# Fused attention and mixture of experts: router logits and values from one matmul per token tile, other slots for the steps around it

## The reference, cut to what matters

```
zn  = (xn - mean) / sqrt(var + eps) * ln_w + ln_b
qkv = zn @ W_qkv + b_qkv                    # 16 heads of 8
s   = xn + softmax(q k^T / sqrt(8)) v @ W_proj + b_proj
logits  = xn @ Wr + br                      # 8 experts
weights = softmax over the two largest logits, 0 elsewhere
ffn = sum over e of weights[e] * (gelu(xn @ W1[e] + b1[e]) @ W2[e] + b2[e])
```

## Time and profile before

| | us |
|---|---|
| median of 3 runs (lowest, highest) | 1032.16 (1031.27, 1032.86) |
| the profiled execution, its own time | 1031.52 |
| its span | 1029.5 |
| TensorE busy (matmul) | 1008.1 |
| ScalarE busy | 859.4 |
| VectorE busy | 842.9 |
| GpSimd busy | 351.1 |

### The profile page before, as it was taken

How to read it: one execution, slowest core, us unless ns; L and a number is a source line. 1 busy time by engine, 2 the same in 40 slices (tenths; PEclk the granted TensorE clock), 3 DMA queues, 4 the chain that set the end, 5 groups by cost and what they waited for, 6 DMA issues and landing times.

```text
span 1029.5 us, 17024 instructions
## 1 busy us (share of the span) xinstructions
PE 1008.1 (98%) x5837; PEld 443.0 (43%) x5869; DVE 842.9 (82%) x1283; ACT 859.4 (83%) x1166; POOL 351.1 (34%) x432
## 2 busy tenths in 40 slices
PE   6999999999999999999999999999999999999998
PEld 4676666666666666667222222222222222222222
DVE  5757878878887887785799999999999999999953
ACT  7877667676767767666999999999999999999985
POOL 5795665656575565746200010001000001000010
PEclk9999999999999999999999999999999999999999
DMA  6542322315132231412421222122221222212113
GB/s 198 131 117 60 103 56 59 102 32 145 31 93 69 57 118 33 113 39 69 116 53 50 55 60 57 42 60 54 54 63 43 58 53 53 59 51 57 26 26 88
DMA packets 102955, 72.11 MB, mean 70 GB/s; under 512 B 25737, under 2 KB 87878, under 8 KB 102870
## 3 DMA queue, kind: packets, MB, share of 16 engines
q1 hardware_dynamic: 102870, 71.04, 26.5%
HBM read 53.12 MB, written 15.59 MB: 67 GB/s over the span
## 4 chain that ended last, share of the span: by engine, by line
PE 87%; DVE 5%; issue 2%; ACT 2%; POOL 0%; another core or an unknown queue 0%; DVEq 0%; ACTq 0%; POOLq 0%
PE psum L1044 22%; PE psum L1004 13%; PE psum L989 10%; PE psum L974 6%; PE psum L934 5%; PE psum L936 5%; PE psum L935 5%; PE psum L952 5%; PE psum L960 4%; PE psum L957 4%; PE psum L958 4%; DVE neg_max_half L1321 1%; DVE neg_max_half L1295 1%; DVE neg_max_half L1291 1%; ACT p_ring L855 1%
## 5 line engine op out<-in xcount | busy, mean ns | idle before, releaser
L855 ACT ACTIVATE p_ring<-psum 128x1024 f32<-128x1024 f32 x512 | 494.5, 1031 | 19.6 <-PE psum L1004 9.1
L1291 DVE TENSOR_REDUCE neg_max_half<-psum 128x2 f32<-128x1024 f32 x240 | 294.3, 1226 | 42.3 <-PE psum L989 34.2
L1044 PE MATMUL psum<-p_ring,v_sb 128*9 128x512 f32 x2048 | 267.6, 594 | 0.2 <-ACT o_sb L846 0.2
L1321 DVE TENSOR_REDUCE neg_max_half<-psum 128x1 f32<-128x512 f32 x304 | 200.0, 685 | 74.9 <-PE psum L974 60.2
L812 ACT ACTIVATE h_hi<-psum,cols 128x512 fp32r<-128x512 f32 x192 | 132.4, 690 | 114.8 <-PE psum L936 114.0
L670 POOL TENSOR_TENSOR h_lo<-h_split,h_hi 128x512 fp32r<-128x512 f32 x128 | 166.2, 1300 | 151.8 <-ACT h_split L815 151.4
L1004 PE MATMUL psum<-q_stack,k_stack 51*128 51x512 bf16 x1024 | 201.2, 385 | 1.3 <-ACT p_ring L855 0.7
L989 PE MATMUL psum<-k_max_stack,q_max_stack 48*128 48x512 bf16 x720 | 182.2, 378 | 1.1
L1004 PEld LDWEIGHTS psum<-q_stack,k_stack 51*128 51x128 bf16 x1024 | 49.1, 92 | 296.6 <-ACT p_ring L855 282.7
L1295 DVE TENSOR_REDUCE neg_max_half<-psum 128x1 f32<-128x512 f32 x240 | 161.2, 672 | 0.0
L624 POOL CAST neg_max_parts<-neg_max_rest 128x16 bf16<-128x16 f32 x32 | 6.5, 203 | 448.4 <-DVE neg_max_rest L1304 448.2
(11 more groups left out here) (121 smaller groups left out, 967.9 us busy)
## 6 DMA issues: line engine op xcount, KB each, us to landing
expert_w_bc<-expert_w_dram SPq DMA_DIRECT2D x64, 256.0 KB, 4.9
k_rows_dram<-qk_parts SPq DMA_DIRECT2D x24, 256.0 KB, 2.8
q_max_stack<-q_rows_dram SPq DMA_DIRECT2D x64, 96.0 KB, 2.5
k_max_stack<-k_rows_dram SPq DMA_DIRECT2D x64, 96.0 KB, 2.5
q_stack<-q_rows_dram SPq DMA_DIRECT2D x64, 96.0 KB, 2.5
k_stack<-k_rows_dram SPq DMA_DIRECT2D x64, 96.0 KB, 2.5
q_rows_dram<-qk_parts SPq DMA_DIRECT2D x8, 384.0 KB, 2.6
xz<-in_L_attn_z_dram SPq DMA_DIRECT2D x8, 256.0 KB, 4.9
```

The costliest lines, as they stand in the source:

```text
L855: act.activation(p_sb[:, n % PR, a, :, :].rearrange("p h t -> p (h t)"), scores_at(s), ACT.Exp, scale=SCALE).then_inc(S("P"), 1)
L1044: i = pe.matmul(o_bank[at:at + VR, :], v_sb[:, b * KT + kt, 2 * (p % PB) + hh, :], p_sb[:, n % PR, a, hh, :], start=(kt == 0), stop=(kt == ...
L1291: dve.tensor_reduce(flat[:, at[0]:at[1] + 1:at[1] - at[0]], psum[:, 5 * TG:7 * TG].rearrange("p (u t) -> p u t", u=2), AX.X, ALU.max, nega ...
L1321: dve.tensor_reduce(mx[:, p % MXR, c, hh * NT + t:hh * NT + t + 1], early_bank[m % 2], AX.X, ALU.max, negate=True).then_inc(S("R"), 1)
```

## The change

From the second group on there is no separate `logits` and no `v`. In slot 12 one matmul per token tile takes `xnT` against `wvr_sb`, 136 columns: `ln_w * W_v` (128) and the router's weights (8). The first tile's result lies in the last 136 columns of b6's bank, the others in b5's. VectorE's `router_top` moves from slot 15 to 14 and takes the first tile's values out right behind its first addition (`values_of(0, 1)`); the other three follow in slot 15. TensorE's `t2` moves from 15 to 17 and waits for that first tile. ScalarE's `z_t` moves from 15 to 18 and `tanh` from 17 to 18, behind it; VectorE's `router_weights` stays in 17. `qk` moves from 18 to 20, its copies from 19 and 21 to 21 and 23, `w_t` from 21 to 23 (its copy from 23 to 25), GpSimd's rests from 21 and 22 to 23 and 25, its thirds from 25 and 26 to 27 and 28, VectorE's `second` from 24 and 25 to 26 and 27. The first group keeps its order and gains three steps: ScalarE scales `W_v` by `ln_w`, TensorE multiplies a broadcast `ln_b` with `W_v` and VectorE adds that to the bias row.

```diff
+        lv_at = 5 * TG - (D + E)
+        lv = psum[:, lv_at:lv_at + TT * (D + E)].rearrange("p (t c) -> p t c", c=D + E)
...
+                return {4: [rsqrt(g, 1)], 8: [rsqrt(g, 2)], 23: [rest(0)], 25: [rest(1)],
+                        27: [third(0)], 28: [third(1)]}
...
+                def value_weights():
+                    act.activation(wvr_sb[:, 0:D], wqkv_sb[:, 2 * D:3 * D], ACT.Copy, scale=col(C_LNW))\
+                        .then_inc(S("wv"), 1)
-                return {7: [normalise], 10: [x_t], 13: [z_scale], 15: [z_t], 17: [tanh], 19: [qk(0)], 21: [qk(1)], 23 if g else 27: [w_t]}
+                if g == 0:
+                    return {7: [normalise], 10: [x_t], 13: [z_scale], 15: [z_t], 17: [tanh], 19: [qk(0)], 21: [qk(1)],
+                            27: [w_t], 28: [value_weights]}
+                return {7: [normalise], 10: [x_t], 13: [z_scale], 18: [z_t, tanh], 21: [qk(0)], 23: [qk(1)], 25: [w_t]}
...
                 def t2():
                     wait(pe, "zn", g, 1, 1)
-                    wait(pe, "vd", g, 1, 0)
+                    if g:
+                        pe.wait_ge(S("vd_first"), g)
...
+                def logits_and_values():
+                    wait(pe, "xh", g, 1, 1)
+                    wait(pe, "kf", g, 1, 0)
+                    if g == 1:
+                        pe.wait_ge(S("wv"), 1)
+                        pe.wait_ge(S("vd"), 1)
+                    for t in range(TT):
+                        m = pe.matmul(lv[:, t, :], xnT[:, t * P:(t + 1) * P], wvr_sb[:, :], start=True, stop=True)
+                    m.then_inc(S("lg"), 1)
+
+                def value_bias():
+                    pe.matmul(b7[:, 0:D], col(C_LNB).broadcast_to([P, P]), wqkv_sb[:, 2 * D:3 * D],
+                              start=True, stop=True).then_inc(S("lnb_v"), 1)
...
                 def qk():
+                    if g:
+                        pe.wait_ge(S("vd"), g + 1)
...
-                return {9: [t1], 12: [logits], 15: [t2], 18: [qk], 21 if g else 26: [w_t], 25: [v]}
+                if g == 0:
+                    return {9: [t1], 12: [logits], 15: [t2], 18: [qk], 26: [w_t], 25: [v], 27: [value_bias]}
+                return {9: [t1], 12: [logits_and_values], 17: [t2], 20: [qk], 23: [w_t]}
...
+                def values_of(t0, t1):
+                    def step():
...
+                        for t in range(t0, t1):
+                            i = dve.scalar_tensor_tensor(
+                                v_sb[:, g * TT + t, :, 0:DH], lv[:, t, 0:D].rearrange("p (h d) -> p h d", h=H),
+                                nwt[:, 4, t:t + 1], bv_bc[:, :].rearrange("p (h d) -> p h d", h=H), ALU.mult, ALU.add)
+                        i.then_inc(S("vd_first" if t0 == 0 else "vd"), 1)
+                    return step
...
+                if g:
+                    return {0: [x_here, spread(0, 1)], 1: [spread(1, 4)], 3: [moments], 12: [low_x],
+                            14: [router_top], 15: [values_of(1, TT)],
+                            17: [router_weights], 18: [router_sum], 19: [router_done],
+                            26: [second(0)], 27: [second(1)]}
                 return {7: [] if g else [normalise_rest], 0: [x_here, spread(0, 1)], 1: [spread(1, 4)], 3: [moments], 12: [low_x], 15: [router_top],
                         17: [router_weights], 18: [router_sum], 19: [router_done],
-                        24: [second(0)], 25: [second(1)], 28: [values]}
+                        24: [second(0)], 25: [second(1)], 28: [values], 29: [value_bias]}
```

More of the change, by code:

```diff
@@ L135, in attention_and_experts @@
         wqkv_sb = fs("wqkv_sb", [P, 3 * D])
-        wr_sb = fs("wr_sb", [P, E])
+        wvr_sb = fs("wvr_sb", [P, D + E])
+        wr_sb = wvr_sb[:, D:D + E]
         bv_bc = fs("bv_bc", [P, D])
@@ L504, in _ @@
             sp_weight(sp, 0)
-            sp.dma_start(wr_sb[:, :], w_r).then_inc(S("wr"), 16)
+            sp.dma_start(wr_sb, w_r).then_inc(S("wr"), 16)
             sp_weight(sp, 1)
@@ L612, in third @@
                     return step
-                return {4: [rsqrt(g, 1)], 8: [rsqrt(g, 2)], 21: [rest(0)], 22: [rest(1)],
-                        25: [third(0)], 26: [third(1)]}
+                if g == 0:
+                    return {4: [rsqrt(g, 1)], 8: [rsqrt(g, 2)], 21: [rest(0)], 22: [rest(1)],
+                            25: [third(0)], 26: [third(1)]}
+                return {4: [rsqrt(g, 1)], 8: [rsqrt(g, 2)], 23: [rest(0)], 25: [rest(1)],
+                        27: [third(0)], 28: [third(1)]}
             def neg_parts(p):
@@ L764, in z_t @@
                     wait(act, "t2", g, 1, 1)
-                    wait(act, "v", g, 1, 0)
+                    if g == 1:
+                        act.wait_ge(S("v"), 1)
+                    wait(act, "k", g, 1, 0)
                     act.activation(znT[:, :], b6[:, :], ACT.Identity, scale=col(C_LNW), bias=col(C_LNB))\
@@ L896, in logits @@
                     for t in range(TT):
-                        m = pe.matmul(b5[:, t * E:(t + 1) * E], xnT[:, t * P:(t + 1) * P], wr_sb[:, :],
+                        m = pe.matmul(b5[:, t * E:(t + 1) * E], xnT[:, t * P:(t + 1) * P], wr_sb,
                                       start=True, stop=True)
                     m.then_inc(S("lg"), 1)
+                def logits_and_values():
+                    wait(pe, "xh", g, 1, 1)
+                    wait(pe, "kf", g, 1, 0)
+                    if g == 1:
+                        pe.wait_ge(S("wv"), 1)
[6 more added lines that the diff above has]
+                              start=True, stop=True).then_inc(S("lnb_v"), 1)
                 def qk():
@@ L971, in early_scores @@
                     pe.wait_ge(S(f"mst{p % 2}"), 64 * (p // 2 + 1))
+                if m == 1:
+                    pe.wait_ge(S("bvn"), 1)
                 if m > 1:
@@ L1173, in router_top @@
                         dve.wait_ge(S("br"), 16)
-                    ch.mark(dve.tensor_tensor(lg[:, :, :], b5[:, 0:TT * E].rearrange("p (t e) -> p t e", e=E),
+                    ch.mark(dve.tensor_tensor(lg[:, :, :], lv[:, :, D:D + E] if g else b5[:, 0:TT * E].rearrange("p (t e) -> p t e", e=E),
                                               br_bc[:, :].unsqueeze(1).broadcast_to([P, TT, E]), ALU.add))
+                    if g:
+                        values_of(0, 1)()
                     ch.sync()
@@ L1227, in values, with value_bias @@
                                       .broadcast_to([P, TT, H, DH]), ALU.add).then_inc(S("vd"), 1)
+                def values_of(t0, t1):
+                    def step():
+                        if t0 == 0:
+                            wait(dve, "lg", g, 1, 1)
+                            wait(dve, "nwt", g, 2, 2)
+                            if g == 1:
+                                dve.wait_ge(S("bvn"), 1)
+                            if g == 2:
+                                dve.wait_ge(S("w_lo"), 2 * E)
+                        for t in range(t0, t1):
[4 more added lines that the diff above has]
+                    return step
+                def value_bias():
+                    dve.wait_ge(S("lnb_v"), 1)
+                    dve.wait_ge(S("vd"), 1)
+                    dve.tensor_tensor(bv_bc[:, :], b7[:, 0:D], bv_bc[:, :], ALU.add).then_inc(S("bvn"), 1)
+                if g:
+                    return {0: [x_here, spread(0, 1)], 1: [spread(1, 4)], 3: [moments], 12: [low_x],
+                            14: [router_top], 15: [values_of(1, TT)],
+                            17: [router_weights], 18: [router_sum], 19: [router_done],
+                            26: [second(0)], 27: [second(1)]}
                 return {7: [] if g else [normalise_rest], 0: [x_here, spread(0, 1)], 1: [spread(1, 4)], 3: [moments], 12: [low_x], 15: [router_top],
                         17: [router_weights], 18: [router_sum], 19: [router_done],
-                        24: [second(0)], 25: [second(1)], 28: [values]}
+                        24: [second(0)], 25: [second(1)], 28: [values], 29: [value_bias]}
             def experts(g):
@@ L1328, in o_zero @@
             def o_zero():
-                dve.wait_ge(S("vd"), NG)
+                dve.wait_ge(S("kf"), NG)
                 dve.memset(o_bank[:, :], 0.0).then_inc(S("o_zero"), 1)
```

## The result

The changed kernel took 1054.05 us (median of 4, 1052.5 to 1055.45) against 1031.78 for the kernel before: ratio 1.0208, interval 1.0188 to 1.0228. It is slower, as forecast, but by 22.3 us in place of 6.6, and outside the range given. Whether by more than 2% the interval leaves open.

A forecast was written before the change was run, and what follows sets the result against it. TensorE, busy 98% of the span at full clock, was taken as the bound. Terms -6.2 + 11.0 + 0.7 + 0.4 + 0.5 + 0.2 = +6.6 us gave a median of 1038.8 us; range 1027 to 1043.

The forecast's parts named there:

- Saving of the merged matmul: TensorE's logits and values in one matmul group of 0.95 us: 0.89 a group, seven groups, 6.2 us less.
- Rival (c): Matmul steps go by their columns, so merging saves nothing: 1032.2 without the tanh wait, 1045.0 with it; chance 0.05.
- The late tanh: tanh in slot 18 holds up VectorE's router_weights; TensorE waits for a maximum in slots 19 or 20: 11.0 us more.
- z_t's 0.70: ScalarE's z_t ahead of tanh in slot 18, taken to delay tanh and so VectorE by 0.70 us.
- rival (b): A draw: slots 14 to 17 already run late, so waiting is about 1 us a group: 1032 to 1033; chance 0.10.
- VectorE's denser queue: Values in slots 14 and 15, second parts of q and k in 26 and 27: small stalls, 0.4 us over six groups.
- First turn and prologue: Group 1's down(16) waiting for low_h(16), 0.7 us; its q and k rows read back late, 0.5; prologue additions, 0.2.
- "nothing" for GpSimd's slots: GpSimd's rests and thirds in slots 23, 25, 27 and 28, three of them free of low_h: no cost.
- The early scores' first rows: Group 1's q and k rows, stored and read back for the first early score, come late: 0 to 2, taken as 0.5 us.
- Rival (a): The gain stays: the late tanh costs TensorE less than 1.0 us a group; 1026.9 with all of it hidden; chance 0.25.

## Why the prediction was right and wrong

- **Saving of the merged matmul**, 6.2: right. 0.88 us a group, its eight steps cost 0.95 to 0.96 (0.95 taken). Rival (c), steps that go by their columns, is out.
- **The late tanh**, 11.0: right in kind, place and, at 12.8, nearly in size, group 5's slot 20 included. Two runs show it, one by putting tanh back and one by moving the instruction that waits. The size was off by two things: L1227 waits for GpSimd as well (0.57 for 0.17), and in group 5 a wait of 2.12 stands where I had 0.5 and 1.0. But z_t's 0.70, which I added up on the way to the 1.9, does not matter: with it gone the wait is the same. VectorE's release comes with the end of GpSimd's low_h(17), which happens to lie near the end of gelu, z_t and tanh; that the 1.9 came out near the 2.15 is in part luck. The lateness of slots 14 to 17 that rival (b) named did come, and took nothing off the wait: without it (router_top and the values one slot later) the waits are 2.11 to 2.16.
- **VectorE's denser queue, "0 to 3 us, I take 0.4"**: the step that failed. It was 7.2 in slots 16 and 17, and 0.8 in slot 29 of group 5 besides. I priced the values alone, called slot 14 a gap, and put router_top's own move there at nothing; beside GpSimd's low_h its last instruction takes 1.14 us longer in five of six groups, and the one ahead of it (L1219) 0.3 to 0.7. The trace of before had the sign of it: L1239 at 1.65 for 0.69, which I used only as a bound elsewhere, and, nearer, an instruction of router_top itself. L1181 took 0.46 to 0.66 us for 0.19 in five groups, each time ending with a low_h of GpSimd, here at 161.30:

```profile
160.87 0.48 DVE L1181 TENSOR_TENSOR router<-logits,top 128x32 f32<-128x32 f32 x1
```

```profile
158.77 2.53 POOL L670 TENSOR_TENSOR h_lo<-h_split,h_hi 128x512 fp32r<-128x512 f32 x2 [3.76 <-ACT h_split L815]
```

- **The granted clock**: the second step that failed. The forecast had no term for it. It gives 6.6 us in the profiled execution. A wait of 2 us was priced at 2 us; in four of six groups it brought 1.6 more.
- **First turn and prologue**, 0.7 + 0.5 + 0.2 less 0.9 saved: 0.5 forecast, 1.3 measured. Group 1's down(16) waited 0.93 longer, inside its bounds; but "nothing" for GpSimd's slots was wrong in the first turn, where the thirds in 27 and 28 leave TensorE waiting 1.6 us longer than before in slot 32.
- The early scores' first rows came 0.2 to 0.3 us late, not 0.5.

The prediction does not derive its range's upper end, 1043. Its terms' upper bounds add up to 16.5 us, 1048.7, and even that is 5.4 short of 1054.05: the one collision with GpSimd in them is low_h's, and none holds a fall of the clock. Rival (a) needed a late tanh of less than 1.0 us a group; it cost 2.1.

## What to carry to other kernels

A step that waits on another engine is priced by what stands behind it in the same queue: put the instruction that waits behind those on which the bounding engine depends, not ahead of them. Before a VectorE step with two SBUF inputs, or a tensor_scalar in SBUF, moves by a slot, look at what GpSimd does in the new slot; a 0.18 us instruction can take 1.3. And where TensorE otherwise runs without a break, an idle stretch can cost more than its length: here 1.6 us more behind four of six waits of 2.1 us.

## What was not expected of the hardware

Where they meet a low_h of GpSimd, the length of L1221 and L1227 is set by its end, not by their own work: 1.32 and 1.24 us for 0.18 and 0.17. Who waits is not fixed: in group 5 L1221 took its 0.18 and GpSimd's pair 0.05 longer. And spare matmuls in an idle stretch of 2 us made the kernel 5.3 us faster, with the granted clock at the 2.4 GHz level throughout the expert stage. In the run with tanh back in slot 17, where waits of up to 1.8 us a group remained in slots 16 and 17, none of them longer than 1.2 in one piece, it did not fall either.
